# Two-layer decoder on one core: the causal mask of the probabilities as a select on GpSimd, with one ring of score banks and paired value products

## What is computed

```python
x = _layernorm(x + _L0_attn_ref(x, ...))          # causal attention, 16 heads of 16
x = _layernorm(x + _L0_xattn_ref(x, ctx_768, ...))  # attention over the 1024 context rows
x = _layernorm(x + _L0_ffn_ref(x, ...))           # soft mixture of 8 experts
x = _layernorm(x + _L1_attn_ref(x, ...))          # causal attention
x = _layernorm(x + _L1_xattn_ref(x, ctx_768, ...))  # attention over the context
x = _layernorm(x + _L1_ffn_ref(x, ...))           # pre-norm, causal attention, pre-norm, top-2 of 8 experts
```

```python
w = jnp.einsum('bhnd,bhmd->bhnm', q, k) * jax.lax.rsqrt(float(D))
w = jnp.where(mask > 0, w, NEG)          # mask: lower triangle
w = jax.nn.softmax(w, axis=-1)
attn = jnp.einsum('bhnm,bhmd->bhnd', w, v)
```

## Time and profile before

| | us |
|---|---|
| median of 3 runs | 3121.71 |
| the runs | 3111.83, 3124.85, 3121.71 |
| the profiled execution | 3118.74 |
| its span, first to last instruction | 3117.0 |
| busy: TensorE products | 2581.8 (83%) |
| busy: VectorE | 1518.0 (49%) |
| busy: ScalarE | 1346.9 (43%) |
| busy: GpSimd | 456.7 (15%) |

### The profile page before, as it was taken

The page is one execution under the profiler, slowest core; times in us unless marked ns, Lnnn a source line. Parts: engine busy times, 40 slices in busy tenths (PEclk is TensorE's granted clock), DMA queues, the critical chain, the costliest instruction groups (busy, mean ns, idle before and its releaser), DMA issues. The chain is left out here.

```text
span 3117.0 us, 47191 instructions
## 1 busy us (share of the span) xinstructions
PE 2581.8 (83%) x15793; PEld 1466.9 (47%) x15794; DVE 1518.0 (49%) x4196; ACT 1346.9 (43%) x2886; POOL 456.7 (15%) x719
## 2 busy tenths in 40 slices
PE   5999899999828889996788889898987996489991
PEld 2555444443314446674455544343434554356771
DVE  2444677888326510022444478777754563322223
ACT  2655356666624421111344446565654553022220
POOL 3222212101110000000122212112022100500003
PEclk8999999999959989998799999999998998589996
DMA  7444555444000022214544465344412332711102
GB/s 203 122 122 126 113 103 98 61 60 72 1 17 1 0 87 76 68 44 152 129 109 120 113 103 73 60 91 63 82 45 67 112 89 73 262 38 34 32 31 88
DMA packets 184547, 259.93 MB, mean 83 GB/s; under 512 B 32952, under 2 KB 106944, under 8 KB 184256
## 3 DMA queue, kind: packets, MB, share of 16 engines
q1 hardware_dynamic: 181264, 248.85, 33.8%
q0 software_dynamic: 3072, 8.39, 0.8%
HBM read 180.71 MB, written 81.53 MB: 84 GB/s over the span
## 5 line engine op out<-in xcount | busy, mean ns | idle before, releaser
L1340 ACT ACTIVATE second_p<-psum 128x512 f32<-128x512 f32 (+3 forms) x1024 | 461.7, 519 | 303.6 <-PE psum L1206 300.4
L1340 ACT ACTIVATE first_p<-psum 128x512 f32<-128x512 f32 (+3 forms) x768 | 365.2, 546 | 196.3 <-PE psum L1206 193.6
L1414 DVE TENSOR_REDUCE second_max_parts<-psum 128x1 f32<-128x512 f32 x512 | 329.0, 685 | 94.9 <-PE psum L1183 93.6
L1414 DVE TENSOR_REDUCE first_max_parts<-psum 128x1 f32<-128x512 f32 x512 | 329.1, 685 | 88.7 <-PE psum L1183 87.6
L1410 DVE CUSTOM_DVE_ANT_0 second_masked<-psum,mask_qk 128x384 f32<-128x384 f32 (+3 forms) x512 | 231.0, 489 | 236.2 <-PE psum L1183 198.6
L1183 PE MATMUL psum<-second_k,second_q 64*128 64x512 f32 (+3 forms) x1024 | 211.1, 408 | 144.9 <-DVE second_max_parts L1414 64.1
L1218 PE MATMUL psum<-second_p,second_v_aug 128*32 128x512 f32 (+3 forms) x2048 | 240.7, 543 | 10.2 <-ACT second_p L1340 10.1
L1196 PE MATMUL psum<-second_q,second_k 64*128 64x512 f32 (+3 forms) x1024 | 227.8, 440 | 15.5 <-ACT second_p L1340 14.3
L1183 PE MATMUL psum<-first_k,first_q 64*128 64x512 f32 (+3 forms) x768 | 161.2, 416 | 62.3 <-DVE first_max_parts L1414 39.2
L1183 PEld LDWEIGHTS psum<-second_k,second_q 64*128 64x128 f32 x1024 | 103.0, 196 | 216.5 <-DVE second_max_parts L1414 102.6
L1206 PE MATMUL psum<-second_shift_T,choose 64*128 64x512 f32 (+3 forms) x1024 | 200.7, 386 | 0.0
(11 more groups left out here) (317 smaller groups left out, 3821.1 us busy)
## 6 DMA issues: line engine op xcount, KB each, us to landing
first_k<-c_k_parts SPq DMA_DIRECT2D x128, 128.0 KB, 5.5
second_q<-a_q_parts SPq DMA_DIRECT2D x256, 64.0 KB, 2.8
second_k<-a_k_parts SPq DMA_DIRECT2D x256, 64.0 KB, 2.8
second_k<-c_k_parts SPq DMA_DIRECT2D x128, 128.0 KB, 5.7
first_q<-a_q_parts SPq DMA_DIRECT2D x128, 64.0 KB, 2.9
first_k<-a_k_parts SPq DMA_DIRECT2D x128, 64.0 KB, 2.9
c_k_parts<-first_held SPq DMA_DIRECT2D x16, 512.0 KB, 3.1
first_q<-c_q_parts SPq DMA_DIRECT2D x128, 64.0 KB, 5.1
```

The costliest lines, as they stand in the source:

```text
L1340: evacuated(act.activation(probs[tile % 2][:, 2 * h + p, q0:SEQ], bank[:, q0:SEQ], ACT.Exp, scale=scale), event)
L1414: evacuated(v.reduce_max(max_parts[n % 2][:, h, p, qt, k0 // BANK:k0 // BANK + 1], bank[:, 0:width], axis=AX_X), event)
```

## The change

It does five things, all in one diff.

1. *The mask.* The four mask products of each score pair go, with the constants `pick` and `mask_kq`. After the exponentials of a pair, POOL sets the probabilities above the diagonal to zero, in place (`cut_future`, an `affine_select` on two heads x 128 queries). In causal layers the values wait for the semaphore `cut` of the tile's second select instead of for the exponentials.
2. *One ring.* All seven banks beside bank 6 are one ring, `SHARED_BANKS`. A filler waits for the use seven banks before, whichever engine reads it; the two semaphores of reads stay.
3. *Values in pairs.* The values of tiles `t - 2` and `t - 1` stand one behind the other, after the scores of `(t, 0)` with `t` even; those of a group's last two tiles after the next group's first scores. There are three `probs` buffers.
4. *POOL's events.* Root, application, bias and the pre-norm's root become four events each, with costs of their own, and are spread among the other pieces; the bias of the output is woven between the projections.
5. *The kept block.* `block_in` is in DRAM. SP stores it (`keep_rows`) and the gate stage loads it back as part of the list of its prefetched transfers, between the 5 MB of `fills` and the gate's weights; POOL waits for it before its additions.

```diff
-S_RING, U_RING, PV_BANK = (0, 1, 2, 3), (4, 5, 7), 6
+SHARED_BANKS, PV_BANK = (0, 1, 2, 3, 4, 5, 7), 6
+PROBS = 3
...
-        pieces += [("stats", slot, 1), ("aggregate", slot, 0), ("apply", slot, 0)]
+        pieces += [("stats", slot, 1), ("aggregate", slot, 0)]
+        pieces += [("root", slot, i) for i in range(4)] + [("apply", slot, t) for t in range(QT)]
...
-        pieces += [("pre_stats", after, 0), ("pre_aggregate", after, 0), ("pre_invert", after, 0),
-                   ("pre_scale", after, 0), ("pre_add", after, 0)]
+        pieces += [("pre_stats", after, 0), ("pre_aggregate", after, 0), ("pre_scale", after, 0)]
+        pieces += [("pre_invert", after, i) for i in range(4)] + [("pre_add", after, 0)]
...
-COST = {"oturn": 450, "xturn": 450, "oproj": 1750, "split": 1750, "value": 1750}
+COST = {"root": 900, "apply": 1250, "bias": 750, "pre_invert": 900, "oturn": 450, "xturn": 450, "oproj": 1750, "split": 1750, "value": 1750}
...
-            if t:
-                plan.append(("values", n, t - 1))
-            elif n:
-                plan.extend([("values", n - 1, layer_of(n - 1).key_tiles - 1), ("drain", n - 1, 0)])
+            if t and t % 2 == 0:
+                plan.extend([("values", n, t - 2), ("values", n, t - 1)])
+            elif t == 0 and n:
+                last = layer_of(n - 1).key_tiles - 1
+                plan.extend([("values", n - 1, last - 1), ("values", n - 1, last), ("drain", n - 1, 0)])
...
-            ring = ring_of(event)
-            banks = S_RING if ring == "S" else U_RING
-            last = 1 if event[0] in ("scores", "unit") else 0
-            wait_for(eng, ring_read[ring], ring_at[ring][event, last] - len(banks) + 1)
+            before = {}
+            for h in range(2 if event[0] in ("scores", "unit") else 1):
+                at = bank_at[event, h] - len(SHARED_BANKS)
+                if at >= 0:
+                    ring, *own = users[at]
+                    before[ring] = ring_at[ring][tuple(own)] + 1
+            for ring, count in before.items():
+                eng.wait_ge(ring_read[ring], count)
...
+                def keep_rows(slot):
+                    sp.wait_ge(applied, QT * (norm_at[before_x(slot)] + 1))
+                    sp.dma_start(slots[slot].copy_to[slot % BATCH].rearrange("(q p) d -> p q d", p=P), x_of(slot)).then_inc(copied, 16)
...
+                def cut_future(event):
+
+                    _, n, (t, p) = event
+                    wait_evacuated(pool, event, 1)
+                    own = probs[value_at[n, t] % PROBS][:, :, t * P:(t + 1) * P].rearrange("x (h p) q -> x p h q", p=2)[:, p, :, :]
+                    pool.affine_select(out=own, in_=own, compare_op=ALU.is_ge, fill=0.0, base=0,
+                                       pattern=[[0, 2], [1, P]], channel_multiplier=-1).then_inc(cut, 1)
...
-                    if layer.causal:
-                        for x in range(2):
-                            for h in range(2):
-                                own = slice(64 * h, 64 * h + 64)
-                                pe.matmul(bank_of(event, h)[:, q0:q0 + 64 * (x + 1)], c.pick[own, x, :],
-                                          c.mask_kq[own, x, 0:64 * (x + 1)], start=False, stop=False)
...
-                    wait_evacuated(pe, ("scores", n, (t, 1)), 1)
+                    if layer.causal:
+                        pe.wait_ge(cut, cut_at[n, t, 1] + 1)
+                    else:
+                        wait_evacuated(pe, ("scores", n, (t, 1)), 1)
...
-                        wait_for(act, value_done, tile - 1)
+                        wait_for(act, value_done, tile - PROBS + 1)
...
-        gate_loads = [(gate_w[:, :, :], a["L1_ffn_gate_W"].rearrange("(k p) e -> p k e", p=P), gate_in),
+        gate_loads = [(rows_in[:, b * QT:(b + 1) * QT, :], block_in[b].rearrange("(q p) d -> p q d", p=P), block_back)
+                      for b in range(BATCH)]
+        gate_loads += [(gate_w[:, :, :], a["L1_ffn_gate_W"].rearrange("(k p) e -> p k e", p=P), gate_in),
...
+                pool.wait_ge(block_back, 16 * BATCH)
```

More of the change, by code:

```diff
@@ L698, in front_pieces @@
     if what == "x":
-        pieces = [("xturn", slot, k) for k in range(DK)] + [("bias", slot, 0)]
-        pieces += [("split", slot, ("q", m, 0)) for m in range(DK)]
-        if not layer.context:
-            pieces += [("split", slot, ("k", m, 0)) for m in range(DK)]
-            pieces += [("value", slot, v) for v in range(QT // 2)]
-        return pieces
+        pieces = [("xturn", slot, k) for k in range(DK)]
+        for m in range(DK):
+            pieces += [("split", slot, ("q", m, 0)), ("bias", slot, m)]
+        if layer.context:
+            return pieces + [("bias", slot, t) for t in range(DK, QT)]
+        for m in range(DK):
+            pieces += [("split", slot, ("k", m, 0)), ("bias", slot, DK + m)]
+        return pieces + [("value", slot, v) for v in range(QT // 2)]
     if what == "k":
@@ L832, in stage_attentions @@
             score_at[n, x] = len(score_at)
+            if slots[n // GROUPS].causal:
+                cut_at[(n, *x)] = len(cut_at)
         elif kind == "values":
             value_at[n, x] = len(value_at)
-        elif kind == "apply":
+        elif kind == "root" and x == 0:
             norm_at[n] = len(norm_at)
@@ L1134, in apply @@
-                def apply(slot):
-                    done = norm_at[slot]
-                    pool.wait_ge(aggregated, QT * (done + 1))
-                    root_of(mean_var[:, :, 1], rstd)
-                    for t in range(QT):
-                        pool.tensor_scalar(x_of(slot)[:, t, :], x_of(slot)[:, t, :], mean_var[:, t, 0:1], rstd[:, t:t + 1],
-                                           ALU.subtract, ALU.mult).then_inc(applied, 1)
-                    after = slot + BATCH
-                    if after < len(slots) and slots[after].copy_to is not None:
-                        pool.wait_ge(applied, QT * (done + 1))
-                        b = slot % BATCH
-                        pool.tensor_copy(slots[after].copy_to[:, b * QT:(b + 1) * QT, :], x_of(slot)).then_inc(copied, 1)
+                    if part == 0:
+                        step(pool.tensor_scalar(near[:, 0, :], variance, LN_EPS, None, ALU.add))
+                        step(pool.tensor_scalar(near[:, 1, :], near[:, 0, :], -0.5, None, ALU.mult))
+                        step(pool.tensor_scalar(y.bitcast(U32), near[:, 0, :].bitcast(U32), -0.5, ROOT_SEED, ALU.mult, ALU.add))
+                        return
@@ new lines, in root_of, with root @@
+                    step(pool.tensor_tensor(square, y, y, ALU.mult))
+                    step(pool.tensor_tensor(square, square, near[:, 1, :], ALU.mult))
+                    step(pool.tensor_scalar(square, square, 1.5, None, ALU.add))
+                    ins = pool.tensor_tensor(y, y, square, ALU.mult)
+                    if part == 3 and done is not None:
+                        ins.then_inc(done, 1)
+                    else:
+                        step(ins)
+                def root(event):
+                    _, slot, part = event
+                    if part == 0:
+                        pool.wait_ge(aggregated, QT * (norm_at[slot] + 1))
+                    root_of(mean_var[:, :, 1], rstd, part)
```

113 lines of the change are left out of this document (55 added, 58 removed).

## The result

The changed kernel takes 3136.76 us (median of 20 runs, 3124.35 to 3145.34), the kernel before 3117.35 us (20 runs): ratio 1.0055, 95% interval 1.0043 to 1.0068. It is slower by half a per cent, and the interval does not reach 1. The forecast was 2928 us, and the time lies above the range's 3060. Its profiled execution took 3131.8 us with a span of 3129.9. One run of a later experiment (e6) took 4262 us at a granted clock of 0.58, where its other six took 3096 to 3109; it moves that median by 0.2 us.

A forecast was written before the change was run, and what follows sets the result against it. TensorE alone was taken to bound the causal layers, TensorE and VectorE nearly together the context layers. Causal -74, context -120 and outside +3 gave -191 us from 3118.74, so 2928 us; range 2815 to 3060 us.

The forecast's parts named there:

- masks to selects, causal: -71 + 35: Causal layers: 71 us gained by removing the mask products, 35 us lost to new waits for selects.
- pairs, stops, ring, causal: -19 - 14 - 7 - 10: Causal layers: gains of 19 us from paired values, 14 and 7 from stops, 10 from the longer ring.
- context layers: 32 groups: -120 us net: gains 25 stops, 60 waits, 16 restarts, 26 pairs; loss 7 new VectorE waits.
- Loads ... I add 12 us: Causal layers: waits for key loads grow by 12 us, as transfers take the same time while groups get shorter.
- (a): Causal layers: POOL's in-order queue becomes the bound, with values waiting for selects; slower, 3181 us, chance 0.11.
- Of the other 75 I take 60: Context layers: of 75 us of TensorE's waits for VectorE left after the long stops, the ring removes 60.
- the 26 us for the pairs: Context layers: values of two key tiles in a row save 0.2 us a pair, 128 pairs, 26 us.
- TensorE alone is the bound: Causal layers: TensorE is the only limit and POOL has room, so time on TensorE's queue counts nearly in full.
- three stops of 4.56 us: Causal layers: stops behind POOL's block of root chain and four applications vanish once it is spread, 14 us gained.
- 14.31 us stop: Causal layers, 2394 to 2408 us: VectorE waits for POOL's root and application; half goes, 7 us gained.
- (b): Context layers: ring brings nothing, VectorE and TensorE still stop each other, only 26 us of pairs remain; 3022 us, chance 0.15.
- (c): Causal layers: TensorE's granted clock falls, 0.83 instead of 0.93, costing 100 us; 3028 us, chance 0.05.

The follow-up runs named there:

- e6: e1 with the two separate rings of banks of the kernel before in place of the one ring; 3105.58 us, ratio 0.9961.
- e4: The kernel before the change, with query and key loads issued ahead of the value load; 3075.01 us, ratio 0.9845.
- e5: e1 with the mask products back on TensorE in place of the selects; 3032.77 us, ratio 0.973.
- e1: The changed kernel with query and key loads issued ahead of the value load, nothing else; 3019.41 us, ratio 0.9679.
- e7: e1 with the values one key tile at a time instead of in pairs, three probs buffers kept; 3039.92 us, ratio 0.9749.
- e10: e1 with VectorE's maxima in the context layers reading only half of each bank; 2985.49 us, ratio 0.9569.

## Why the prediction was wrong

The sum again, each term against the stages. The parts of the change are read at equal loads (e4, e5, e1), the loads as what the order costs in each kernel. All are differences of single profiled executions: e4 to e1 is 66.8 us by the spans and 55.6 by the medians, so the terms below are good to some 10 us.

| term | booked | measured |
|---|---|---|
| masks to selects, causal: -71 + 35 | -36 | -22.6 (e5 to e1) |
| pairs, stops, ring, causal: -19 - 14 - 7 - 10 | -50 | -11.2 (e4 to e5) |
| context layers | -120 | -38.2 (e4 to e1) |
| key loads | +12 | +78.1 (117.4 after, 39.3 before) |
| start | 0 | +19.9 (e4 to e1) |
| the rest | +3 | -13.1 |
| sum, by the spans | -191 | +12.9 |

**The step that failed in sign** is "Loads ... I add 12 us". The argument was that store, load and landing take the same time while groups get shorter. They started later: the term came out at 78 us by the stages and 68 by the medians. The prediction asked who waits for the selects and answered "the pair of values"; it did not follow the augmentation, which the change puts behind the selects on POOL, to the value load that waits for it and the 16 loads behind that. I had even named POOL's strict order in rival (a), but priced only the values' wait. Without this term the change is a gain of 1.8% (e1 against e4: 55.6 us by the medians).

**The largest miss in size** is the context layers, 82 us. The length of single groups, from shift turn to shift turn, tells which of its terms came. One group of c0 that carries no pieces, in the kernel before, in the changed kernel and in e7 (one ring, single values); then a group of c0 that carries an output projection, before and after:

```profile
638.37:664.74 26.37, 23.91 (x172) 10.27 (x169) 21.80 (x41) 17.78 (x34) 1.29 (x1) 1.00 0.48 71
674.11:699.18 25.07, 23.81 (x170) 10.68 (x169) 20.94 (x41) 17.72 (x35) 1.29 (x1) 1.00 0.51 74
643.44:667.87 24.43, 23.85 (x172) 10.43 (x168) 21.25 (x41) 17.72 (x34) 1.29 (x1) 1.00 0.58 76
...
553.96:585.15 31.19, 28.79 (x197) 13.77 (x193) 23.87 (x46) 18.99 (x36) 1.29 (x1) 1.00 0.42 60
590.19:624.00 33.81, 30.17 (x194) 14.63 (x193) 24.23 (x51) 18.81 (x37) 9.23 (x20) 0.95 0.36 56
```

From e4 to e1 the 31 groups that can be measured so fall into three kinds. The three groups of c1 with the long stops are 32 us shorter (booked: 25). They are also short in e6, so it is not the ring that cures them. The 11 groups in which TensorE has no pieces are 15.4 us shorter, 1.4 each. With the ring alone (e7) it is 2.0 each: TensorE's idle time in such a group goes from 2.5 to 0.6 us, about as much as the group gets shorter. Over 32 groups that would be 65 us, about the 60 booked for the ring; the pairs take back 0.6 us a group, where 26 us of gain were booked for them. The other 17 groups, which carry pieces or begin or end a layer, are 9 us longer: there the waits for VectorE's maxima fell by 7 us, and waits for key loads of the context layers, for the transposed outputs (`oT`, `xT`) and for the shift came in their place. So in the context layers the step that failed is "Of the other 75 I take 60", which lets the waits go in every group as they go in one without pieces, and the 26 us for the pairs. The waits for VectorE did fall, from 103 to 36 us, 7 of them before the units (under 20 was the sign of being right). VectorE's share of a context window went from 80 to 77%, where the prediction wanted over 85%. Leaving out half of each maximum still gave 22 us (e10), and the slower pairs of 0.50 instead of 0.39 us did not go.

**The causal terms.** The select was right in price: 0.41 us (384 in 154.6 us) where I took 0.5, and its waits of 35 us were an over-estimate: 2.6 us in the changed kernel, 11.8 in e1. The two hand-overs booked at 0.1 us each took 0.07 (ScalarE to the select, median of 220) and 0.06 us (select to values); no run isolates the 0.3 us of fill.

```profile
L1107 POOL TENSOR_SCALAR_AFFINE_SELECT second_p<-second_p 128x256 f32<-128x256 f32 x256 | 103.1, 408 | 383.4 <-ACT second_p L1360 380.1
L1107 POOL TENSOR_SCALAR_AFFINE_SELECT first_p<-first_p 128x256 f32<-128x256 f32 x128 | 51.5, 407 | 179.7 <-ACT first_p L1360 178.9
```

But 71 us of masks taken off TensorE's queue gave 22.6 by the stages and 13 by the medians: "TensorE alone is the bound" was too strong. The waits of e5 and e1 show what a freed TensorE meets. From e5 to e1 those for ScalarE's exponentials go from 11 to 24 us, those for the maxima of the causal layers (line 1430) from 12 to 25, those for the shift from 19 to 23 and those for selects from 0 to 12: some 41 us of the 71. The three stops of 4.56 us in a1 are gone, 14 us as booked, and a1 is 14.8 us shorter from e4 to e5. The 14.31 us stop became one of 9.42 us and one of 4.12 us, for VectorE's maxima and for `second_rows`; together 13.5 us, where I had booked a gain of 7. From e4 to e5 ring and pairs brought nothing more in these layers; that one ring is worth 45 us in them beside the pairs (e6) says that pairs with two rings would have cost time.

**The start** was left out. I had noted that one start-up wait stays, but not that sharing a ring makes units wait for another engine's evacuation, hence for a store.

**The rivals.** (a) fell: POOL is 40 and 27% busy in the two causal windows, values wait 2.6 us. (b) was nearest for the context layers in size, 82 of its 94 us were missing, but not in mechanism: in the groups without pieces the ring alone brought what was booked. (c) happened in a2: 0.81 instead of 0.93; in a0 and a1 the clock is 0.89 and 0.90, from 0.94 and 0.93. It came through the loads, not through waits for selects, and e1, which has every select, is back at 0.92. (TensorE: Matmul & The Clock Gate of the Trainium skill, section on oscillation, warns of idles between groups of products; the traces here agree for stops of 1.4 to 5.5 us in 12 of a2's 16 groups.) None of the five had the mechanism that decided the sign.

What stays open: why the key-load stops set the clock so much lower in a2 than in a0 at a similar length, and most of the 13 us gained in the rest of the program. From e4 to e1, 12 us of it lie between the last measured group of c0 and the start of a1, and 5 of them are lost again with two rings (e6) and with single values (e7). The kept block in DRAM cost nothing that shows: from a2's last shift turn to the end it is 513.9 us before and 510.0 after. The spreading of POOL's events had no run of its own.

## What to carry to other kernels

When work moves to an in-order queue, list every instruction that now stands behind it, and follow each to the transfers it releases, not only to the consumer that the diff makes wait; a load that waits for a buffer should not stand ahead of loads that do not need that buffer. Sharing a ring between two streams joins their stalls: look for the one place where a stream is held by something slow, above all at the start. A wait that goes in one kind of group need not go in another: before booking it for all, measure group by group, and look at what else stands in the groups that carry other work. And add up the whole idle time, since a wait for one engine can be replaced by a wait for another.

## What the runs showed of the hardware

A select of 128 x 256 f32 took 0.407 to 0.408 us, against 0.282 us for the one of 128 x 128: doubling the width added only 0.126 us. The 16 loads behind the value load took SP 7.5 us from the first issue to the last (2513.20 to 2520.66), 0.5 us each, half of a group of 14.45 us, so the last of them is issued that much later than the first. And the price of a stop lies partly after it: for the same products in a2, TensorE was busy 205.4 us with 12 stops for keys in 16 groups (38.6 us), at a granted clock of 0.81, and 178.4 us with three stops (3.6 us), at 0.92.
